# Earlier first weight loads, other filler blocks, and a bias row split at the start of attention, in an eight-core convolution and attention layer

## What is computed

```python
xn = _layernorm(x)
# attention branch
c = conv1d(xn, conv_w, 3 taps, 4096 -> 3072) + conv_b
q, k, v = split(c)                       # 1024 columns each
qh = q @ wq + bq; kh = k @ wk + bk; vh = v @ wv + bv
p = softmax(causal(qh * scale @ kh.T))   # within blocks of 128 tokens
s = ((p @ vh) @ wo + bo) @ proj_w + proj_b
# router branch
scores = softmax(xn @ router_weight.T + router_bias)
w_dense, w_sum = top 8 of scores, and their sum
g = silu(xn * w_sum + w_dense @ expert_bias)
return x + s * g
```

## Time and profile before

| | |
|---|---|
| median of the runs | 1843.4 us |
| the profiled execution | 1832.8 us, of it the span of the slowest core (core 7) 1831.3 us |
| spans of the eight cores | 1811.7 to 1831.3 us |
| busy, share of the span | TensorE 88%, VectorE 22%, ScalarE 21%, POOL 12% |
| mean granted TensorE clock | 0.886 of full speed on core 7 (0.886 to 0.891 on all) |

### The profile page before, as it was taken

How to read it: one execution, slowest core, us unless ns; L and a number is a source line. 1 busy time by engine, 2 the same in 40 slices (tenths; PEclk the granted TensorE clock), 3 DMA queues, 4 the chain that set the end, 5 groups by cost and what they waited for, 6 DMA issues and landing times.

```text
span 1831.3 us, 21285 instructions; the slowest of 8 cores (1811.7 to 1831.3 us)
## 1 busy us (share of the span) xinstructions
PE 1613.8 (88%) x9136; PEld 818.3 (45%) x9136; DVE 396.6 (22%) x644; ACT 384.2 (21%) x453; POOL 228.2 (12%) x180
## 2 busy tenths in 40 slices
PE   7678799999999999999999999998866765779994
PEld 7678644444444444444444444433333443423221
DVE  2877200000000000000000000000055255137777
ACT  1443000000000000000000000029754345233442
POOL 0000011111111111111111111100000000024435
PEclk9789899999999999999999999999955555579886
DMA  6999365665656566565665656662400001643454
GB/s 145 211 242 195 50 81 71 79 76 74 81 71 79 74 77 80 70 81 73 77 78 72 80 72 79 77 107 47 93 1 1 1 1 21 118 104 142 151 167 183
DMA packets 230834, 163.83 MB, mean 89 GB/s; under 512 B 74691, under 2 KB 222403, under 8 KB 226499
## 3 DMA queue, kind: packets, MB, share of 16 engines
q0 software_dynamic: 155472, 92.97, 38.7%
q1 hardware_dynamic: 75270, 69.50, 14.6%
HBM read 220.69 MB, written 16.78 MB: 130 GB/s over the span
## 4 chain that ended last, share of the span: by engine, by line
PE 68%; DVE 10%; DMA 9%; ACT 5%; SPq 4%; issue 3%; DVEq 0%; ACTq 0%; POOLq 0%
PE pCv L650 55%; DMA AL<-x 5%; PE pWO L931 4%; DMA AL<-pw 4%; PE pPr L999 3%; SPq L432 2%; ACT AL L712 2%; DVE AL L805 1%; PE pQ L734 1%; DVE tRs L797 1%; ACT L712 1%; DVE AL L1048 1%; DVE tStat L326 1%; PE pLgt L310 1%; SPq L437 1%
## 5 line engine op out<-in xcount | busy, mean ns | idle before, releaser
L650 PE MATMUL pCv<-AL 128*128 128x512 bf16 x4608 | 1000.6, 379 | 0.0
L650 PEld LDWEIGHTS pCv<-AL 128*128 128x128 bf16 x4608 | 449.4, 98 | 550.8
L783 DVE TENSOR_REDUCE tSc<-pS 128x1 f32<-128x512 f32 x32 | 21.8, 680 | 1199.5 <-PE pS L776 1199.5
L593 POOL DMA_DIRECT2D AL<-cw x144 | 125.9, 875 | 1064.6 <-PE pCv L650 871.0
L665 ACT ACTIVATE AL<-pCv,tCbT 128x512 bf16<-128x512 f32 x48 | 29.1, 688 | 889.2 <-PE pCv L650 889.2
L999 PE MATMUL pPr<-AL 128*128 128x512 bf16 x448 | 118.8, 413 | 10.3 <-DVE AL L1048 10.3
L931 PE MATMUL pWO<-AL 64*128 64x256 bf16 x512 | 109.8, 416 | 5.7 <-DVE AL L857 5.7
L310 PE MATMUL pLgt<-tI 128*128 128x128 bf16 x1712 | 99.0, 221 | 7.2 <-DMA tOnes<-ones 7.2
L310 PEld LDWEIGHTS pLgt<-tI 128*128 128x128 bf16 x1712 | 97.3, 99 | 8.2 <-issue 7.5
L931 PEld LDWEIGHTS pWO<-AL 64*128 64x128 bf16 x512 | 74.4, 146 | 40.3 <-issue 6.6
L470 PE MATMUL pLgT<-AL 128*64 128x128 bf16 x768 | 55.9, 247 | 40.7 <-DMA AL<-AL 40.7
(11 more groups left out here) (97 smaller groups left out, 909.9 us busy)
## 6 DMA issues: line engine op xcount, KB each, us to landing
AL<-cw POOLq DMA_DIRECT2D x144, 512.0 KB, 5.8
AL<-x SPq DMA_DIRECT2D x16, 2048.0 KB, 12.6
out<-AL SPq DMA_DIRECT2D x8, 2048.0 KB, 8.1
AL<-pw POOLq DMA_DIRECT2D x8, 1024.0 KB, 8.2
AL<-wq POOLq DMA_DIRECT2D x1, 2048.0 KB, 18.2
AL<-wk POOLq DMA_DIRECT2D x1, 2048.0 KB, 15.5
AL<-wv POOLq DMA_DIRECT2D x1, 2048.0 KB, 15.1
AL<-wo POOLq DMA_DIRECT2D x1, 2048.0 KB, 15.0
```

The source lines that it names most:

```text
L593: sCWs[gi % 4].add(e.dma_start(out=cwr[:, gi % 4, :].rearrange("p (g f) -> p g f", g=8), in_=d_cw[s, g].rearrange("g p f -> p g f")), 16)
L650: ins = e.matmul(p_cv[:, 512 * (bs + 2 * sub + hf): 512 * (bs + 2 * sub + hf) + 512], lhsT, xnTh[:, o:o + 512], start=(step == 0), stop=(s ...
```

## The change

Four edits. The first four convolution weight loads go to a buffer `cwrB` of their own, in the columns of the x slot xB, and wait for the last normalisation reads of x tile 7 (hiB written, cHI at 16, and ScalarE's last copy, cXNA at 32) and no longer for the last router matmul; from the fifth on the loads go to the old ring. The filler block at the start grows from 600 to 900 matmuls; the one ahead of the convolution shrinks from 200 to 120. The fp32 bias row and its two bf16 parts lie on partition 64 now (the parts in columns whose partitions 0 to 63 hold other data), with a row of ones on partition 64 for their matmuls. And the split of the bias row, which stood behind the last output evictions, is emitted between the v projection and attention on ScalarE and VectorE.

```diff
-        t_ones2 = sb("tOnes2", [2, 128], BF16)
+        t_ones2 = sb("tOnes2", [65, 128], BF16)
...
+        cwrB = bfv(A_XB, 4 * 2048).rearrange("p (r f) -> p r f", r=4)
...
-        pbf32 = f32v(A_X6A, 4096, 1)
-        pbhi = bfv(A_PBHI, 4096, 1)
-        pblo = bfv(A_PBLO, 4096, 1)
+        pbf32 = AL[64:65, A_X6A:A_X6A + 8192].bitcast(F32)
+        pbhi = AL[64:65, A_CWR:A_CWR + 4096]
+        pblo = AL[64:65, A_CWR + 4096:A_CWR + 8192]
...
             e.memset(t_eps[:], EPS)
+            e.memset(t_ones2[64:65, :], 1.0)
...
             e.wait_ge(sCST2.h, 48)
-            warm(e, 600)
+            warm(e, 900)
...
-                warm(e, 200)
+                warm(e, 120)
...
-            sCST2.add(e.dma_start(out=t_ones2[:], in_=d_ones2), 16)
+            sCST2.add(e.dma_start(out=t_ones2[0:2, :], in_=d_ones2), 16)
...
                 if gi == 0:
+                    e.wait_ge(cHI.h, 16)
+                    e.wait_ge(cXNA.h, 32)
+                if gi == 4:
                     e.wait_ge(cPEr.h, 1)
                 if gi >= 4:
                     e.wait_ge(cPEc.h, gi - 3)
+                dst = cwrB if gi < 4 else cwr
                 sCWs[gi % 4].add(e.dma_start(
-                    out=cwr[:, gi % 4, :].rearrange("p (g f) -> p g f", g=8),
+                    out=dst[:, gi % 4, :].rearrange("p (g f) -> p g f", g=8),
                     in_=d_cw[s, g].rearrange("g p f -> p g f")), 16)
...
-                                lhsT = cwr[:, gi % 4, 256 * k + 128 * sub:
-                                           256 * k + 128 * sub + 128]
+                                lsrc = cwrB if gi < 4 else cwr
+                                lhsT = lsrc[:, gi % 4, 256 * k + 128 * sub:
+                                            256 * k + 128 * sub + 128]
...
         EV3ALL = 80
 
+        @AC
+        def _(e):
+            e.wait_ge(sPB32.h, 16)
+            e.wait_ge(cPE3.h, 16)
+            cPB.add(e.copy(pbhi[0:1, :], pbf32[0:1, :]), 1)
+
+        @DV
+        def _(e):
+            e.wait_ge(cPB.h, 1)
+            cPB.add(e.tensor_sub(pblo[0:1, :], pbf32[0:1, :], pbhi[0:1, :]), 1)
...
-            @AC
-            def _(e):
-                e.wait_ge(sPB32.h, 16)
-                e.wait_ge(cPE5.h, 32)
-                cPB.add(e.copy(pbhi[0:1, :], pbf32[0:1, :]), 1)
-
-            @DV
-            def _(e):
-                e.wait_ge(cPB.h, 1)
-                cPB.add(e.tensor_sub(pblo[0:1, :], pbf32[0:1, :], pbhi[0:1, :]), 1)
...
-                                     t_ones2[0:1, :],
+                                     t_ones2[64:65, :],
                                      pbhi[0:1, 512 * seg:512 * seg + 512],
```

## The result

The changed kernel is slower. Its median is 1860.5 us against 1843.4 us before; over the comparable runs the ratio is 1.0079, with a 95% interval from 1.0063 to 1.0096, so +14.6 us (11.6 to 17.7). I had forecast 1844 in a range of 1836 to 1856. The difference is under the 2% that the prediction took for no change, but clear of the noise. The profiled execution of the changed kernel took 1860.3 us, its slowest core 1858.8.

What follows compares the result with a forecast made beforehand. Bound: 1000 us of convolution matmuls, untouched; only three seams could move. -4.6 + 0 + 1.8 + 8.7 - 5.4 = +0.5 us on 1832.8 gives 1833.3, plus 10.6 to the median: 1844 us, range 1836 to 1856.

Steps and rivals of the forecast that it cites:

- the even split: Tile 7's low transposes and early weight loads share DMA engines evenly: landing at 186.0 instead of 180, costing +1.8 us.
- my upper bound of 194: Tile 7's low transposes stand behind all four weight loads, land at 194, and VectorE takes the logits 9.8 us late.
- the slack: Before tile 7's router matmuls: 4 us in hand, said to absorb part of a late transpose landing.
- 900 fillers at the start: First filler block, 600 to 900: 17.1 us more, covered by TensorE's 17.95 us idle before router tile 0; 0 us.
- My near row: First stage: a pair of transposes took 12.68 us beside a 2 MB x load, 4.93 us without one.
- the collision at the pw loads: Start of last projection: x tile 0's load amid the pw loads slowed both sides, two pitches taking 22.77 instead of 17.3 us.
- The fillers: Block ahead of the convolution, 200 to 120: 80 matmuls of 57 ns leave the path, -4.6 us; the first block 0.
- The bias row at attention's start: ScalarE's copy and VectorE's subtraction come before the first row maximum, 1331.2 instead of 1322.45: +8.7 us.
- the late row: Rival at attention's start: bias row lands late, +13.5 instead of +8.7 us, total +5.3, 1849 us; chance 0.08.
- 1852 with 3 us of spread: Rival, transposes lose to the weight loads: +9.8 instead of +1.8 us, 1852; with run-to-run spread, range end 1856; chance 0.17.
- The pw loads: Start of last projection: x tile 0's load leaves the stretch of eight pw loads, pitch 8.67 us, gaining -5.4 us.
- The base: Whole kernel: sum added to the profiled execution of 1832.8 us, then shifted 10.6 us to the median of 1843.4.

Runs made afterwards that it cites:

- the hidden split: Kernel before with the changed fillers, no early loads, bias row loaded at the convolution's end and split by VectorE alone during the v projection; ratio 0.9973.
- the second profile: The kernel before, unchanged, profiled a second time: 1844.9 us, where the first profiled execution had 1832.8.

## Why the prediction was wrong

**The weight loads beside the transposes (failed, and it decides).** The step that failed is the even split of the DMA engines between the weight loads and the low transposes of tile 7: landing at 186.0, a cost of 1.8 us, and 9.8 as the far end. The runs showed a landing at 196.1 on core 7, and 13.6 us of time for the early loads alone, 11.3 us of it at the convolution's start in the mean of the cores; in the whole change 15 to 16 us there. Four things were wrong in that step. First, the even split. I split the *time* of the engines evenly, so that 6 us of transposes would take 12. The queues of the changed kernel on core 7, with packets, MB and share of the engines' time (q0 is the weight loads, q1 the transposes), over 176 to 196.1 us:

```profile
q0 software_dynamic: 4160, 2.10, 82.6%
q1 hardware_dynamic: 4160, 1.05, 46.5%
```

And over 188 to 190 us:

```profile
q0 software_dynamic: 484, 0.25, 89.2%
q1 hardware_dynamic: 485, 0.12, 46.3%
```

The transposes' queue in the kernel before, over 176 to 178 us, with no load beside it:

```profile
q1 hardware_dynamic: 1894, 0.48, 106.8%
```

From 184 to 194 the two queues' counts agree within five packets in every window of 2 us: for each packet of the loads one of the transposes is moved. A load's packet carries twice the bytes and takes about twice the engine time, so the transposes don't get half of their rate but about a quarter, 485 packets in 2 us instead of 1894. And since the low pair has as many packets as the four loads together, 4160, it is through only when they are: 4160 packets at 485 in 2 us are 17 us, from 178 to 195. The measured landing, 196.1, is next to my upper bound of 194. The Trainium skill ("DMA: Bandwidth & Descriptors", "Queues, rings and completion order") says that an engine takes turns between its queues a packet at a time. The trace agrees in its equal counts, though it doesn't show single turns; I had read the rule as a share of time.

Second, the upper bound was added to tile 7 alone. The wait also lets the clock fall: in the mean tile 7 took 7.1 us instead of 5.5, and the block of 120 fillers, which starts at the low clock (granted 0.50 up to 224 on core 7), 7.8 instead of 6.9; that makes 33.0 us from tile 7's start to the convolution with early loads, 30.5 without.

Third, I took the slack from core 7 alone (4 us) and from the kernel with 600 fillers. In the mean of the cores tile 7 started 2.9 us after the low pair's landing there, and with 900 fillers only 1.1 us after it (181.2 against 180.2, without early loads). One early load shows it: the low pair lands 4.8 us later (184.9 against 180.2), and tile 7 starts 3.8 us later in the mean (185.0 against 181.2), not 0 to 2.

Fourth, I took the edits for independent. In the whole change tile 7 starts at 194.8 in the mean, with the early loads alone at 189.7; the 5 us lost there are those that the fillers give back behind it (33.0 us to the convolution instead of 38.1), so both kernels reach it at 227.8. Half of the 5 us lies ahead of the low pair: it is issued at 172.6 in the mean instead of 170.1, since with 900 fillers at the start the high transposes of tile 7 go out 1.6 us later and take 5.4 to 6.6 us of the queue instead of 4.3 to 5.4 (in all runs with 900 fillers, with early loads or without). The other half lies in the landing, 22.1 us after the issue instead of 19.6: the low pair goes out behind the loads instead of just ahead of them. That the order counts is borne out by the run with the loads behind the high transposes; why 900 fillers delay and lengthen the high pair stays open.

**My near row was the right one, and I talked it down.** A pair of transposes beside an x load took 12.68 us instead of 4.93. I set it aside since that load stood in the same queue. The measured pair took 14.59. And I had the collision at the pw loads the wrong way round, as if the transfer on SP's queue had lost least there: x tile 0 landed 13.9 us after its issue instead of the 7.9 of x tile 1, 1.8 times as long, while the two pw pitches beside it were 11.4 us instead of 8.67, 1.3 times.

**The fillers (right behind tile 7, partly given back ahead of it).** -4.6 predicted; from tile 7 to the convolution -3.8 by the fillers alone, -4.9 with the bias row (30.5 us instead of 35.4). The block of 120 took 6.9 us on most cores without early loads, as foreseen, and 7.6 in the mean of the run with the fillers alone. The clock at the convolution's start held (granted 1.00 from 226 on, on core 7 of the changed kernel). 900 fillers at the start were to cost nothing at all; tile 7 starts 0.8 us later with them in the mean of six profiles, and in the whole change they cost more, as said. Their end was nearly as foreseen: tile 0 began at 62.59 on core 7, 2.2 us later than before, with its matmuls done in 7.15 instead of 7.81 us, and tile 1 was already waiting for transposes again (3.48 us).

**The bias row at attention's start (right).** +8.7 predicted; measured from the convolution's start 8.9 alone, 9.6 in the full change, and from the row's issue 8.7 in the full change. The landing was the smallest part: on five or six of the eight cores the row was there when ScalarE came free, at most 2.7 us after its issue, and on the others it held ScalarE by 1.1 to 1.6 us (landing after 3.5 to 4.0 us, where I had 3.1). The other parts are those of the sum: 1.28 + 3.60 on ScalarE, 4.42 on VectorE. Two bounds of the prediction were added up a little wrong: the late row comes to 13.8 us by its own numbers, not 13.5, and 1852 with 3 us of spread is 1855, not 1856; neither decides anything.

**The pw loads (right mechanism, a little large).** -5.4 predicted; -4.6 for the bias row alone, -3.1 in the changed kernel, -3.5 with the hidden split. The pitch without the x tile's collision is not 8.67 but 8.8 to 9.0 us: (1631.80 - 1568.70)/7 = 9.0 on core 7 after. I had taken one interval of one core for it.

**The base (unseen).** My sum was made against an execution of 1832.8 us and shifted by 10.6 us to the median, and I said nothing on where these 10.6 us come from. They are the last stage: in that execution three of four pairs had entered it more than 6 us apart. The time is that of the slowest core, so as soon as one pair is in step, some 10 us are added (cores 6 and 7 took 201.9 and 198.7 us there, 211.9 and 210.8 in the second profile). A part of it stood in the spans of the cores that I had (1811.7 to 1831.3).

**The account.** Against the mean of the two profiles before: +11.3 (convolution later: +16.0 for the loads in this company, -4.7 for the fillers), +9.6, -3.1, -0.5, and +5.0 in the last stage, together +22.5 in the mean span. The ratio says +14.6 (11.6 to 17.7). Without the last stage's +5.0 it is +17.5. That the +5.0 is a chance of the profiles is shown by the spans on record: the mean span of the cores is 1845.8 us over seven executions of the changed kernel and 1828.3 over 52 of the kernel before, +17.5 as well. So the change doesn't put more pairs in step, as far as these executions show. The time of the slowest core, which the ratio compares side by side, moved by 3 us less than the mean span; the 52 ran beside other runs, and of the executions that ran beside the changed kernel no core spans are on record, so this rest stays open.

## What to carry to other kernels

A load that isn't needed sooner is not free to issue sooner: look at what is in flight at the new time, and when it is short pieces such as DMA transposes, count packets on both queues, not bytes or busy time, and see who is issued first. The smaller transfer pays for the larger packets of the other. A small job moved off one end of an in-order engine costs its whole length where both ends of a serial chain wait for it; put it where that engine idles (here VectorE under the v projection, 25 us ahead). And before a sum of a few us is trusted, take the difference between the profiled execution and the median apart: a stage with two forms can be larger than every term of the sum.

## What the runs showed of the hardware

The two cores of a pair (0 and 1, 2 and 3, and so on) slow each other in a stage that loads and stores 2 MB a tile on each: most x loads land in 11.6 to 12 us when the two are 6 us or more apart (one tile of a core in about 13), in 12 to 13.5 us at 4.5 to 6 us apart, and in 13 to 16 us when they are closer. A pair that is close mostly stays close (0.6, 0.9, 0.9, 0.9, 1.2, 1.7 us over six tiles in the second profile of before). The Trainium skill ("HBM Reference", "Specifications (TRN2)") says that the two cores of a domain share its bandwidth; the pairs fit that, though no trace here measures the memory itself, and they add that it comes as two forms of one program.

DMA transposes on SP's queue beside casting loads on POOL's: the two queues move equal numbers of packets (478 to 493 each in every 2 us from 184 to 194, core 7 of the changed kernel), and the transposes fall from 1894 packets in 2 us to about 485.

Loads with a cast, issued one at a time on POOL's queue, came at a pitch of 9.0 us for 2 MB read; two in flight at 41.4/7 = 5.9 us each. Only the wait for the previous load's landing was taken away between the two.
